# One semaphore increment per group of matmuls, and the Exp moved behind the copies of attention's output

## What is computed

```
x: (16, 4096, 1024) f32
# attention over channels, in windows of 256 positions with step 128
qkv = x @ W_qkv + b_qkv                     # 16 heads of 64
qw, kw, vw = windows of q, k, v             # (b, h, window, 64, 256)
attn = softmax(einsum('bhndw,bhnew->bhnde', qw, kw) * 64**-0.5)   # 64 x 64
o = einsum('bhnde,bhnew->bhndw', attn, vw)  # 31 windows of 256, laid end to end,
o = o.reshape(...)[:, :4096]                # cut to the first 4096 positions
x = layernorm(x + o @ W_out + b_out)
# feed-forward with int weights (scaled by 1/127), 1024 -> 3072 -> 1024
h = silu(x @ wg.T) * (x @ wu.T)
x = layernorm(x + h @ wd.T)
```

## Time and profile before

| | us |
|---|---|
| two runs | 3416.26 and 3819.32, median 3617.79 |
| the profiled execution, its time | 3420.22 |
| its span, slowest core (core 7) | 3418.7 |
| spans of the eight cores | 3399.8 to 3418.7 |
| PE busy, of the span | 2963.1 (87%) |
| ACT busy | 1252.2 (37%) |
| DVE busy | 935.3 (27%) |
| POOL busy | 182.8 (5%) |

### The profile page before, as it was taken

How to read it: one execution, slowest core, us unless ns; L and a number is a source line. 1 busy time by engine, 2 the same in 40 slices (tenths; PEclk the granted TensorE clock), 3 DMA queues, 4 the chain that set the end, 5 groups by cost and what they waited for, 6 DMA issues and landing times.

```text
span 3418.7 us, 61504 instructions; the slowest of 8 cores (3399.8 to 3418.7 us)
## 1 busy us (share of the span) xinstructions
PE 2963.1 (87%) x23572; PEld 1995.2 (58%) x23572; DVE 935.3 (27%) x1750; ACT 1252.2 (37%) x2721; POOL 182.8 (5%) x324
## 2 busy tenths in 40 slices
PE   0878777687875673899999999999999999999997
PEld 0344444334443331677777777777777777777775
DVE  0344444334442441121221222222122222222221
ACT  0245445434442453143342332333433433323323
POOL 1011111101111100000000000000000000000000
PEclk9999999899997896899999999999999999999998
DMA  7134444333444424611110110111111111101100
GB/s 127 46 94 124 96 118 118 99 90 98 122 107 119 111 91 156 204 38 38 50 41 35 50 44 34 48 44 40 42 44 50 38 38 50 44 32 50 44 32 25
DMA packets 77216, 245.71 MB, mean 72 GB/s; under 512 B 8576, under 2 KB 8576, under 8 KB 76928
## 3 DMA queue, kind: packets, MB, share of 16 engines
q0 software_dynamic: 43744, 138.96, 15.1%
q1 hardware_dynamic: 33184, 102.81, 9.2%
HBM read 175.16 MB, written 102.76 MB: 81 GB/s over the span
## 4 chain that ended last, share of the span: by engine, by line
PE 59%; ACT 0%; DMA 0%; DVE 0%; SPq 0%; issue 0%; POOL 0%; ACTq 0%; DVEq 0%; POOLq 0%
PE psum_qkv L1044 20%; PE psum_O L1025 10%; PE psum_S L1054 10%; PE psum_TR L1054 10%; PE psum_O L1029 10%; DMA wuT<-wuT_scr 0%; DVE y2pre L1099 0%; ACT y L1209 0%; ACT y2sq L1192 0%; ACT y2sq L1189 0%; SPq L989 0%; SPq L981 0%; ACT L1189 0%; DVE h_bf L1075 0%; ACT l2ln L1205 0%
## 5 line engine op out<-in xcount | busy, mean ns | idle before, releaser
L1044 PE MATMUL psum_qkv<-y1fm_sb,wgT 128*128 128x256 bf16 x6144 | 797.9, 273 | 19.3 <-DMA y1fm_sb<-y1fm_scr 19.3
L1044 PEld LDWEIGHTS psum_qkv<-y1fm_sb,wgT 128*128 128x128 bf16 x6144 | 601.7, 98 | 246.6 <-issue 19.5
L1139 ACT ACTIVATE sg_bf<-psum_qkv 128x256 bf16<-128x256 f32 x768 | 293.7, 382 | 1189.6 <-PE psum_S L1054 673.4
L1025 PE MATMUL psum_O<-wdT,h_bf 128*128 128x512 bf16 x1536 | 582.1, 379 | 0.6 <-DVE h_bf L1075 0.6
L1029 PE MATMUL psum_O<-wdT,h_bf 128*128 128x512 bf16 x1536 | 582.2, 379 | 0.0
L1054 PE MATMUL psum_S<-y1fm_sb,wuT 128*128 128x256 bf16 x3072 | 398.9, 273 | 7.0 <-DMA wuT<-wuT_scr 7.0
L1054 PE MATMUL psum_TR<-y1fm_sb,wuT 128*128 128x256 bf16 x3072 | 399.0, 273 | 0.0
L1075 DVE TENSOR_TENSOR h_bf<-psum_TR,sg_bf 128x256 bf16<-128x256 f32 x384 | 163.1, 425 | 795.3 <-PE psum_O L1025 673.0
L1075 DVE TENSOR_TENSOR h_bf<-psum_S,sg_bf 128x256 bf16<-128x256 f32 x384 | 163.1, 425 | 760.0 <-PE psum_O L1025 717.7
L523 PE MATMUL psum_qkv<-wqkv_bf,x_fm 128*128 128x512 bf16 x816 | 315.3, 386 | 49.2 <-DVE q_tm L556 43.5
L1054 PEld LDWEIGHTS psum_S<-y1fm_sb,wuT 128*128 128x128 bf16 x3072 | 300.8, 98 | 42.6 <-issue 7.5
(11 more groups left out here) (145 smaller groups left out, 2404.6 us busy)
## 6 DMA issues: line engine op xcount, KB each, us to landing
xr<-x SPq DMA_DIRECT2D x64, 512.0 KB, 3.6
y1dbg<-y_f POOLq DMA_DIRECT2D x64, 512.0 KB, 3.0
y1r<-y1dbg SPq DMA_DIRECT2D x64, 512.0 KB, 4.2
out<-y POOLq DMA_DIRECT2D x64, 512.0 KB, 2.9
y1fm_scr<-y1fm_stage POOLq DMA_DIRECT2D x8, 2048.0 KB, 7.9
y1fm_sb<-y1fm_scr SPq DMA_DIRECT2D x32, 512.0 KB, 3.2
xt_bf<-x POOLq DMA_DIRECT2D x34, 256.0 KB, 9.3
wqkv_bf<-wqkv POOLq DMA_DIRECT2D x8, 768.0 KB, 26.9
```

The source lines that it names most:

```text
L1025: b.inc(t_.matmul(down_ps[:, 1024 * rs:1024 * rs + 512], lhsT, wdT[:, hc, 0:512], start=(hc == 0), stop=(hc == 23), skip_group_check=True) ...
L1044: b.inc(t_.matmul(gate_ps[hsl], wgT[:, hc, 128 * dc:128 * (dc + 1)], y1fm_sb[:, gsl, dc, :], start=(dc == 0), stop=(dc == 7)), "T", 1)
L1139: b.inc(a.activation(sg_bf[:, hsl, :], gate_ps[hsl], AF.Silu), "A", 1)
```

## The change

Two edits.

1. In nearly every group of PE instructions only the last one keeps its increment: all transposes (L287, L320, L413, L632), the S burst, the AT burst, the O burst, the gate and up groups, and the down matmuls, where one of four keeps it. In the q, k, v passes and in the projection the two bias matmuls at the end keep theirs, and the 16 others lose it.
2. ACT's Exp is moved behind the eight copies, and the tokens are computed accordingly. The layer norm's tokens stay.

The diff, cut to its core (the same form is applied in each place named above):

```diff
@@ emit_qkv_pass (the projection alike)
                         for c in range(8):
                             lhsT = x_fm[:, sl, c, :]
-                            b.inc(t_.matmul(psum_qkv[:, 0:512],
-                                            lhsT, wqkv_bf[:, c, 1024 * p:1024 * p + 512],
-                                            start=(c == 0), stop=False), "T", 1)
+                            t_.matmul(psum_qkv[:, 0:512],
+                                      lhsT, wqkv_bf[:, c, 1024 * p:1024 * p + 512],
+                                      start=(c == 0), stop=False)
...
@@ the O burst (S, AT and the transposes alike)
                                 for par in range(2):
-                                    b.inc(t_.matmul(
+                                    mm = t_.matmul(
                                         psum_O[64 * par:64 * par + 64, dst0:dst0 + 64],
                                         lhsT,
                                         at_bf[:, 128 * hp + 64 * par:128 * hp + 64 * par + 64],
                                         start=True, stop=True,
-                                        skip_group_check=True), "T", 1)
+                                        skip_group_check=True)
+                                    if hp == 7 and c4 == 3 and par == 1:
+                                        b.inc(mm, "T", 1)
...
@@ tokens of a step
                 abase = [b.cnt["A"]]
-                off_exp = 1
-                off_oe = 2 if have_w1 else 1
+                off_exp = 9 if have_w2 else 1
...
-                    oevac_done[gw] = ("A", abase[0] + off_oe + 7)
+                    oevac_done[gw] = ("A", abase[0] + 8)
...
-                                b.wait(t_, "T", ("A", abase[0] + off_oe + max(c, 1 + 4 * k2)))
+                                b.wait(t_, "T", ("A", abase[0] + 1 + max(c, 1 + 4 * k2)))
...
@@ ACT's part of a step
-                        if w1gw is not None:
-                            b.wait(a, "A", ssub_done[w1gw])
-                            b.wait(a, "A", scale_done.get(w1gw - 1))
-                            b.inc(a.activation(aexp[:, :], ssub[:, :], AF.Exp, scale=0.125),
-                                  "A", 1)
                         if w2ctx is not None:
                             gw, s_, n = w2ctx
                             b.wait(a, "A", o_mm_done[gw])
...
                                     AF.Copy), "A", 1)
+                        if w1gw is not None:
+                            b.wait(a, "A", ssub_done[w1gw])
+                            b.wait(a, "A", scale_done.get(w1gw - 1))
+                            b.inc(a.activation(aexp[:, :], ssub[:, :], AF.Exp, scale=0.125),
+                                  "A", 1)
...
@@ gate (up alike)
                     for dc in range(8):
-                        b.inc(t_.matmul(gate_ps[hsl], wgT[:, hc, 128 * dc:128 * (dc + 1)],
-                                        y1fm_sb[:, gsl, dc, :],
-                                        start=(dc == 0), stop=(dc == 7)), "T", 1)
+                        mm = t_.matmul(gate_ps[hsl], wgT[:, hc, 128 * dc:128 * (dc + 1)],
+                                       y1fm_sb[:, gsl, dc, :],
+                                       start=(dc == 0), stop=(dc == 7))
+                        if dc == 7:
+                            b.inc(mm, "T", 1)
```

More of the change, by code:

```diff
@@ L286, in _ @@
                 for c in range(8):
-                    b.inc(t_.transpose(tr_slice(bi, 128 * c, 128 * (c + 1)),
-                                       xt_bf[:, xsl, 128 * c:128 * (c + 1)],
-                                       ident_sb[:, :]), "T", 1)
+                    mm = t_.transpose(tr_slice(bi, 128 * c, 128 * (c + 1)),
+                                      xt_bf[:, xsl, 128 * c:128 * (c + 1)],
+                                      ident_sb[:, :])
+                    if c == 7:
+                        b.inc(mm, "T", 1)
             tx_done[gt2] = b.tok("T")
@@ L412, in _ @@
                     for j, (src_sl, _dst, _comb) in enumerate(batch):
-                        b.inc(t_.transpose(tr_slice(bi, 128 * j, 128 * (j + 1)),
-                                           w_in_bf[:, sl, src_sl[0]:src_sl[1]],
-                                           ident_sb[:, :]), "T", 1)
+                        mm = t_.transpose(tr_slice(bi, 128 * j, 128 * (j + 1)),
+                                          w_in_bf[:, sl, src_sl[0]:src_sl[1]],
+                                          ident_sb[:, :])
+                        if j == len(batch) - 1:
+                            b.inc(mm, "T", 1)
                 tw_tok = b.tok("T")
@@ L592, in _ @@
                                         start=(j == 0), stop=(j == 1),
-                                        skip_group_check=True), "T", 1)
+                                        skip_group_check=True)
+                                    if hp == 7 and par == 1 and j == 1:
+                                        b.inc(mm, "T", 1)
                     s_mm_done[gw1] = b.tok("T")
@@ L631, in _ @@
                                 b.wait(t_, "T", evac_half[((gt, 2), 1)])
[L632 to L634 removed]
+                            mm = t_.transpose(tr_slice(vbi, 128 * c, 128 * (c + 1)),
+                                              v_tmp[:, sl3, 128 * c:128 * (c + 1)],
+                                              ident_sb[:, :])
+                            if c == 7:
+                                b.inc(mm, "T", 1)
                     tvmm_done[gt] = b.tok("T")
@@ L725, in _ @@
                                 lhsT = attn_out[:, c, rb:rb + 128]
-                                b.wait(t_, "T", ("A", abase[0] + off_oe + max(c, 1 + 4 * k2)))
-                                b.inc(t_.matmul(pj[:, 0:512], lhsT,
-                                                wout_bf[:, c, 0:512],
-                                                start=(c == 0), stop=False,
-                                                skip_group_check=True), "T", 1)
-                                b.wait(t_, "T", ("A", abase[0] + off_oe + max(c, 3 + 4 * k2)))
-                                b.inc(t_.matmul(pj[:, 512:1024], lhsT,
-                                                wout_bf[:, c, 512:1024],
-                                                start=(c == 0), stop=False,
-                                                skip_group_check=True), "T", 1)
+                                b.wait(t_, "T", ("A", abase[0] + 1 + max(c, 1 + 4 * k2)))
+                                t_.matmul(pj[:, 0:512], lhsT,
+                                          wout_bf[:, c, 0:512],
+                                          start=(c == 0), stop=False,
+                                          skip_group_check=True)
+                                b.wait(t_, "T", ("A", abase[0] + 1 + max(c, 3 + 4 * k2)))
+                                t_.matmul(pj[:, 512:1024], lhsT,
+                                          wout_bf[:, c, 512:1024],
+                                          start=(c == 0), stop=False,
+                                          skip_group_check=True)
                             b.inc(t_.matmul(pj[:, 0:512], ones128[:, :],
@@ L1024, in _ @@
                         lhsT = h_bf[:, hsl, 128 * rs:128 * (rs + 1)]
-                        b.inc(t_.matmul(down_ps[:, 1024 * rs:1024 * rs + 512],
-                                        lhsT, wdT[:, hc, 0:512],
-                                        start=(hc == 0), stop=(hc == 23),
-                                        skip_group_check=True), "T", 1)
-                        b.inc(t_.matmul(down_ps[:, 1024 * rs + 512:1024 * (rs + 1)],
-                                        lhsT, wdT[:, hc, 512:1024],
-                                        start=(hc == 0), stop=(hc == 23),
-                                        skip_group_check=True), "T", 1)
+                        t_.matmul(down_ps[:, 1024 * rs:1024 * rs + 512],
+                                  lhsT, wdT[:, hc, 0:512],
+                                  start=(hc == 0), stop=(hc == 23),
+                                  skip_group_check=True)
+                        mm = t_.matmul(down_ps[:, 1024 * rs + 512:1024 * (rs + 1)],
+                                       lhsT, wdT[:, hc, 512:1024],
+                                       start=(hc == 0), stop=(hc == 23),
+                                       skip_group_check=True)
+                        if rs == 1:
+                            b.inc(mm, "T", 1)
                 down_done[(g, hc)] = b.tok("T")
@@ L1053, in _ @@
                     for dc in range(8):
-                        b.inc(t_.matmul(up_ps[hsl], wuT[:, hc, 128 * dc:128 * (dc + 1)],
-                                        y1fm_sb[:, gsl, dc, :],
-                                        start=(dc == 0), stop=(dc == 7)), "T", 1)
+                        mm = t_.matmul(up_ps[hsl], wuT[:, hc, 128 * dc:128 * (dc + 1)],
```

(4 more changed lines are left out.)

32 lines of the change are left out of this document (16 added, 16 removed).

## The result

The changed kernel takes 3379.83 us (median of 9 runs, 3375.51 in the fastest) where the kernel before takes 3418.26 on the same chips (median of 8). The ratio is 0.9888 with a 95% interval of 0.9875 to 0.9902: 1.1% less, some 38 us, against the 32.4 us forecast.

A forecast was written before the change was run, and what follows sets the result against it. Attention-stage PE waits, lengthened by queued O-burst increments and a low clock, were taken as the time to regain. From 3420.2 us, -21.6 (tail) + 0.7 (table load) - 11.5 (clock) = -32.4 gave 3388; 8-in-10 range 3368 to 3412.

The forecast's parts named there:

- likeliest case: The forecast itself: O burst's tail gone and the clock helping, 3388 us, own range 3376 to 3394, chance 0.52.
- Where the gain is, and through which instruction: Attention stage, O burst: its late increments delay copy L334 and the chain to the projection; 21.6 us over 27 windows.
- 0.80 us per window: O burst to projection: 0.51 us excess lag of L334 plus 0.29 from a shorter burst; bounds 0.51 and 1.06.
- The burst's own 0.29: O burst's 64 matmuls no longer braked by queued increments: 1.29 us of intervals shrink by 0.29 us.
- Nothing for the long matmuls: qkv, projection, feed-forward: increments do not queue and cost no issue time, 0; rival of a further 31 us, chance 0.08.
- The argument from the spacing at the low level: Projection matmuls at low clock start 427 ns apart, just 512 columns, no gap despite increments; so no fixed price each.
- The S burst, 0: S burst's lag is taken from negmax, and nothing on PE waits for it before the next step: 0.
- The table load in the gap: ACT's 1.28 us load falls before the copies, making them 0.22 us later; hidden in 27 windows, +0.7 us over three.
- The clock, -0.5 us in 23 windows: Windows with two short preparation jobs: a shorter gap before the projection leaves less low-clock time, -11.5 us in all.
- The prediction's outer bound, -1.12: Clock gain per window: all like the better kind, -0.56, and a step further still, another -0.56.
- the tail without the clock (3399): Rival: the increment tail goes but the clock gives nothing, 3399, or 3412 with all windows of the worse kind; chance 0.26.
- the slower rival: Low clock lasts through the whole projection, 121 us slower, 3520; decided by 4 more low-level matmuls per window; chance 0.03.

The follow-up runs named there:

- the first run: Kernel before with 63 of the O burst's 64 increments removed, only the last kept, nothing else changed; ratio 0.989 (0.9858 to 0.9922).
- the fill of 512: Changed kernel with one added DVE fill of 512 bf16 elements per partition ahead of the y transpose copy L338; 3403.0 us, ratio 0.9964 to the kernel before.
- the run with every second increment: Changed kernel with an increment on every second matmul of the O burst, 32 in all; ratio 0.9895 (0.9875 to 0.9914) to the kernel before.
- the delay runs: Changed kernel with DVE fills added ahead of copy L338: one of 512 elements (ratio 0.9964), two of 1024 (1.0133), one of 820 (1.0004).

## Why the prediction was right

The forecast was 3388 us and 32.4 us less than before; it came to 3380 and 38. Its likeliest case is the one that happened, and the steps stand as follows.

- *Where the gain is, and through which instruction.* Right: the O burst alone, through L334 in the windows with jobs (with 63 increments removed from the kernel before the gain is all there, with them put back it is gone, and a fill of the same length in DVE's way undoes it).
- *0.80 us per window.* Measured 2.72 - 1.86 = 0.86 at L334 and 6.65 - 5.79 = 0.86 at the projection. The burst's own 0.29 was exact (1.49 to 1.20). The missing 0.06 is the lag taken as the normal one: 0.17, from the transposes of the jobs, where the y transposes are followed after 0.11, with their own increments on them (the first run) or not. That the transposes show no excess lag, so 0, holds only once the burst's queue is gone; with it in place the y transposes' increments are 0.18 us of the lag.
- *Nothing for the long matmuls.* Right, 1.0002 (0.9992 to 1.0012). The argument from the spacing at the low level held.
- *The S burst, 0.* Right in its effect. Its lag went from 0.43 us to 0.17, and nothing came of it (the first run keeps the 32 increments and has the whole gain):

```profile
738.11 0.45 PE L593 MATMUL psum_S<-k_tm,q_tm 128*64 128x64 bf16 x16 [0.15 <-DVE k_tm L564]
...
738.73 0.69 DVE L607 TENSOR_REDUCE negmax<-psum_S 128x8 f32<-128x512 f32 x1 [0.77 <-PE psum_S L593]
```

- *The table load in the gap.* Right: it lies between "O done" and the first copy in 32 steps, the copies are 0.14 us later than before (0.22 forecast), hidden in the windows with jobs, and the two windows without jobs that can be compared are 0.13 us longer each (0.22 forecast). What the prediction did not see is that the longer gap of such a window can cost a step of the clock as well. The gap is now

```profile
1179.31 1.20 PE L702 MATMUL psum_O<-at_bf,v_fm 128*64 128x64 bf16 x64 [1.32 <-DVE at_bf L684]
...
1180.59 1.28 ACT L792 ACT_TABLE_LOAD   x1 [7.91 <-PE psum_O L702]
...
1182.69 0.38 PE L738 MATMUL psum_O<-wout_bf,attn_out 128*128 128x512 bf16 x1 [1.63 <-ACT attn_out L792]
```

  3.38 us from the burst's start to the projection, at a clock of 1.00; with 4.52 us, in the kernel before with Exp moved, it fell to 0.95. The length alone doesn't decide. With the fill of 512, one such window has the same gap of 3.38 us and 0.95, 1.7 us longer than the next, and in the run with every second increment two windows have gaps of 3.71 us, one 31.45 us long at 1.00 and one 33.15 at 0.95:

```profile
1202.99:1235.81 32.82, 26.12 (x227) 12.66 (x227) 12.87 (x20) 17.02 (x38) 1.81 (x3) 0.95 0.33 129
```

- *The clock, -0.5 us in 23 windows.* Right in sign, and of the terms the one that was most mis-sized. The 23 windows with short jobs became 36.3 us shorter together, 1.58 us each; less the chain's 0.86 that leaves 0.72 us each, 16.5 us in sum instead of 11.5. In the first sequence the settled windows went from a mean of 35.84 to 34.13 to 34.5, in the second from 35.4 to 34.15. With each of the eight cores set against itself the 23 windows became 33 to 41 us shorter, 37.2 in the mean, so the size doesn't hang on the two cores shown. The prediction's outer bound, -1.12 (all windows like the better kind, and a step further), held, and the kernel took part of the further step: windows at 32.84 us and a clock of 1.00 appeared. The delays say the same from the other side: 0.54 us in the chain cost 1.14 us of window, 0.86 us cost 1.7 (34.13 to a mean of 35.83).
- *The sum.* In the two profiled executions, 3420.2 and 3377.1 us, core 7 against core 4, the difference is 43; 36.3 come from the 23 windows, 0.7 from the last window of the first sequence, 2.3 from the four windows behind them in which wdT is made (three became 0.7 to 2.6 us shorter and one 1.9 us longer, where the forecast put each down at 0.80 us less), 1.5 from the rest of the second sequence; some 2 us lie before the first burst.

The two main errors, 0.06 us in the chain and 0.22 us in the clock for each window, lie on the same side, so the sum didn't come near by errors that cancel. Of the rivals, the tail without the clock (3399) fell short by the clock's part, and the slower rival's condition, four more matmuls at the low level, did not arise: fewer were. A delay of the chain costs 1.6 to 2.1 times its length, as the delay runs show, and the rows say of what it is made: about the delay itself, and the step of the clock in more of the windows. What stays open is what decides which windows take that step. Nor was a variant tried in which the table load is taken out of the gap while Exp stays behind the copies.

## What to carry to other kernels

Mark only the last of a burst of short matmuls: look for bursts whose matmuls are issued faster than increments are served (here 15.8 against 34.2 ns), and price the increments by how late the first reader on the path to the next wait of PE starts, not by the length of the queue. On the long matmuls of this kernel, 256 and 512 columns, the increments were free, so there was nothing to win by tidying them. Where PE's wait lets its clock fall, shortening the wait can be worth more than the time cut from it, and moving the work that fills the wait (here to behind the first half of the projection, with enough staging buffers) brought 5.0% with the change in it, where the change alone brought 1.1%.

## What the runs showed of the hardware

- Increments of a burst issued 15.8 ns apart were served 34.2 ns apart, a matmul without one took 8.3 ns between two that had one, and after about 47 matmuls PE was held to the queue's pace.
- The increments of the instructions behind a burst stand in the same queue: seven increments on the transposes more, 0.18 us later.
- ACT's table load of 1.28 us starts only when the semaphore wait of the step's first ACT instruction is over, even when that instruction is a copy; moved behind such a wait it becomes part of the path.
- A delay of 0.86 us cost 1.7 us per window where it also brought every second window from a granted clock of 0.95 to 0.91; one of 1.14 us cost 1.13 us where the clock stayed at 1.00.
